# Issuing the last chunk's output projection and layer norm among the FFN matmuls of the chunk ahead of it

## The reference

```python
xn = _layernorm(x, axis=-1)
s = _L0_attn_ref(xn, L0_attn_w_qkv, L0_attn_w_out)      # global attention, 16 heads of 16
g = _silu(_L0_ffn_ref(xn, ...))                         # two local layers, below
x = x + s * g

def _layer(x, wqkv, qs, ksc, wo, lg, lb, w1, b1, w2, b2):   # applied DEPTH = 2 times
    h = shift_token(x)                       # the second half of the features comes from the token before
    q, k, v = split(h @ wqkv)                # 8 heads of 64
    q, k = rotary_xpos(l2norm(q) * qs, l2norm(k) * ksc)
    o = local_attention(q, k, v)             # windows of 128 tokens, each sees itself and the one before
    x = x + o @ wo                           # output projection
    h = shift_token(x)
    mu = h.mean(-1, keepdims=True)
    var = h.var(-1, keepdims=True)
    h = (h - mu) / jnp.sqrt(var + 1e-05) * lg + lb
    a, g = jnp.split(h @ w1 + b1, 2, axis=-1)
    x = x + (a * gelu(g)) @ w2 + b2          # hidden width 682: five tiles of 128 and a tail of 42
    return x
```

## Time and profile before

| what | us |
|---|---|
| median of 3 runs | 2339.86 (2337.14 to 2340.36) |
| the profiled execution's own time | 2328.96 |
| its span, first to last instruction | 2327.2 |
| mean granted TensorE clock | 0.971 of full speed |
| TensorE busy | 2195.7 (94%) |
| VectorE busy | 1621.7 (70%) |
| ScalarE busy | 1380.5 (59%) |

### The profile page before, as it was taken

One profiled execution on the slowest core, in us unless ns is written; L12 is line 12 of the kernel. 1 busy time (PEld: TensorE's weight loads), 2 busy tenths in 40 slices (PEclk: granted clock), 3 DMA queues, 4 the chain that ended last, 5 costly groups with the idle time before them and its releaser, 6 DMA issues. The chain is left out here.

```text
span 2327.2 us, 43427 instructions
## 1 busy us (share of the span) xinstructions
PE 2195.7 (94%) x14592; PEld 1288.5 (55%) x14592; DVE 1621.7 (70%) x3789; ACT 1380.5 (59%) x2551; POOL 610.5 (26%) x490
## 2 busy tenths in 40 slices
PE   7869999999999979899999999899999999999976
PEld 4533333333333336566666666666666676676644
DVE  5768999999999936655666666556666656666534
ACT  2215888888888845555655555555555565565533
POOL 3521200000000024333332333332432333333201
PEclk9977999999999989999999999999999999999988
DMA  4585122211112022200000000000100000000303
GB/s 135 183 252 159 52 64 65 65 56 60 57 53 63 29 80 103 88 10 1 1 0 0 0 0 0 27 1 10 36 1 1 1 0 0 0 0 0 108 1 109
DMA packets 76984, 108.96 MB, mean 47 GB/s; under 512 B 14204, under 2 KB 49360, under 8 KB 76752
## 3 DMA queue, kind: packets, MB, share of 16 engines
q1 hardware_dynamic: 76864, 107.30, 14.4%
HBM read 68.74 MB, written 43.95 MB: 48 GB/s over the span
## 5 line engine op out<-in xcount | busy, mean ns | idle before, releaser
L669 DVE TENSOR_REDUCE maxima<-ps_m 128x1 f32<-128x512 f32 x1024 | 629.1, 683 | 20.7 <-PE ps_m L549 16.6
L737 ACT ACTIVATE probs<-ps_st 128x1024 f32<-128x1024 f32 x512 | 521.1, 1025 | 161.7 <-PE ps_st L576 142.6
L549 PE MATMUL ps_m<-k_st,q_st 48*128 48x512 f32 x1024 | 392.4, 466 | 19.9 <-DMA k_st<-ks 15.6
L1355 ACT ACTIVATE l_probs<-l_probs,l_neg_max 128x256 f32<-128x256 f32 x512 | 254.0, 498 | 194.5 <-DVE l_neg_max L1514 194.5
L576 PE MATMUL ps_st<-q_st,k_st 50*128 50x512 f32 x1024 | 367.5, 444 | 2.0 <-DMA q_st<-max_rows 1.6
L592 PE MATMUL ps_o<-probs,v_st 128*32 128x256 f32 x4096 | 322.1, 392 | 0.1
L1514 DVE CUSTOM_DVE_ANT_1 l_probs<-ring,l_mask 128x256 f32<-128x256 f32 x384 | 140.0, 421 | 198.5 <-PE ring L1123 198.0
L576 PEld LDWEIGHTS ps_st<-q_st,k_st 50*128 50x128 f32 x1024 | 154.5, 186 | 194.0 <-issue 173.8
L1334 ACT COPY p_turned<-ring 128x512 f32<-128x512 f32 x256 | 140.4, 599 | 163.7 <-PE ring L1083 163.6
L1042 POOL TENSOR_SCALAR clipped<-sumsq 128x16 f32<-128x16 f32 x64 | 16.2, 253 | 766.9 <-DVE sumsq L1481 766.9
L549 PEld LDWEIGHTS ps_m<-k_st,q_st 48*128 48x128 f32 x1024 | 166.7, 190 | 53.3 <-DVE maxima L669 31.5
(11 more groups left out here) (156 smaller groups left out, 3864.7 us busy)
## 6 DMA issues: line engine op xcount, KB each, us to landing
qs<-split SPq DMA_DIRECT2D x16, 512.0 KB, 3.5
ks<-split SPq DMA_DIRECT2D x16, 512.0 KB, 5.1
q_st<-qs SPq DMA_DIRECT2D x64, 128.0 KB, 2.5
k_st<-ks SPq DMA_DIRECT2D x64, 128.0 KB, 3.1
o<-o_sb SPq DMA_DIRECT2D x32, 256.0 KB, 2.3
hidden<-o SPq DMA_DIRECT2D x17, 256.0 KB, 6.6
x_in<-in_L_attn_x_dram SPq DMA_DIRECT2D x8, 512.0 KB, 5.6
v<-v_sb SPq DMA_DIRECT2D x16, 256.0 KB, 4.7
```

Source lines behind the costliest of these rows:

```text
L549: nc.tensor.matmul(bank(base, use)[:, :], q_st[u][r, qt * P:(qt + 1) * P], k_st[u][r, h * CH:(h + 1) * CH], start=True, stop=True).then_in ...
L669: nc.vector.tensor_reduce(maxima[:, par, side(e), tile + e // 4, e % 2:e % 2 + 1], bank(base, k + e)[:, :], AX_X, ALU.max).then_inc(m_used, 1)
L737: nc.scalar.activation(probs[:, kt % 4, j, :], ps_st[j][:, :], ACT.Exp, scale=float(G_DIM) ** -0.5).then_inc(exp_done, 1)
L1355: nc.scalar.activation(probs[:, head, :], probs[:, head, :], ACT.Exp, bias=neg_max[:, head:head + 1], scale=-1.0, accum_out=total[:, head: ...
```

## The change

For body 17 (called late) the projection, the mean and the variance are issued in body 16, into `ps_q`, `ps_k`, `ps_v` and `l_ps_o`, which attention no longer uses there. Their other operands also get new places, all of them attention's: `mid` becomes a view of `l_probs`, `centred` becomes `qk_n`, the squares go to `k_ring`, and the features go to `h` instead of `f_high`/`f_low`. The counts of uses of the `ffn` banks are lowered by the two that fall away (`nth`). ScalarE's table preload goes in body 16 window 2 and in body 17. The arithmetic is the same.

```diff
+        late_banks = (ps_q, ps_k, ps_v, ps_o)
+        l_mid = probs.rearrange("p h n -> p (h n)")[:, 0:KD * (1 + CH)].rearrange("p (k n) -> p k n", k=KD)
+        l_centred, l_squares = qk_n[:, :, :], k_ring[:, 0:KD, :]
+        def late(g):
+            return isinstance(g, int) and g == LAST + 1
+        def nth(g, bank, use):
+            return (g - 2) * USES[bank] + use - (2 if late(g) else 0)
...
+                def late_fill(n, operands):
+                    for k, (a, b) in enumerate(operands):
+                        mm = nc.tensor.matmul(late_banks[n][:, :], a, b, start=(k == 0), stop=(k == len(operands) - 1))
+                    mm.then_inc(late_ready, 1)
+                def late_output():
+                    g = LAST + 1
+                    pe.wait_ge(o_out, WPC * (g - 1))
+                    pe.wait_ge(roped, WPC * LAST)
+                    for m in range(KD):
+                        late_fill(m, [(wt.wo[:, p, m * P:(m + 1) * P], o_ring[:, g % 2, p, :]) for p in range(HEADS // 2)])
+                def late_mean():
+                    pe.wait_ge(v_out, WPC * LAST)
+                    pe.wait_ge(late_mid, KD)
+                    late_fill(2, [(wt.mean_w[:, :], x) for x in shifted(l_mid)])
+                def late_variance():
+                    pe.wait_ge(sq_dev, LAST)
+                    late_fill(3, [(wt.mean_w[:, :], l_squares[:, k, :]) for k in range(KD)])
...
                         if forward and w == 2:
                             hidden_tile(g, lf, 3)
+                        if last_but_one and w == 2:
+                            late_output()
+                        if last_but_one and w == 3:
+                            late_mean()
                         if forward and w == 3:
                             down(g, lf, 0)
+                        if last_but_one and w == 3:
+                            late_variance()
...
-                        if w >= 2 and forward:
+                        if w >= 2 and forward and (mid_ or isinstance(g, int) and g == LAST and w == 3):
                             nc.scalar.preload_act_table_set(EXP_LN)
...
-                        if forward and w == 0:
+                        if forward and w == 0 and not late(g):
                             inverse_deviation(g)
+                        if isinstance(g, int) and g == LAST and w == 3:
+                            square_deviations(g + 1)
+                            inverse_deviation(g + 1)
...
+                        if last_but_one and w == 3:
+                            add_attention(g + 1, n + 1)
...
+                        if last_but_one and w == 3:
+                            centre(g + 1)
                         if forward and w == 3:
                             add_ffn(g, lf, n, 0)
+                        if last_but_one and w == 3:
+                            scale(g + 1, lf)
+                            shift(g + 1, lf)
+                        if forward and w == 3:
                             add_ffn(g, lf, n, 1)
                             carry(g, n)
```

More of the change, by code:

```diff
@@ L1186, in body @@
                 def body(g, la, lf, before_hidden=None):
+                    last_but_one = isinstance(g, int) and g == LAST
                     for w in range(WPC):
@@ L1541, in centre @@
-                def centre(g):
-                    dve.wait_ge(ffn_ready[0], (g - 2) * USES[0] + MEAN + 1)
-                    nc.vector.scalar_tensor_tensor(out=centred[:, 0, :], in0=ffn[0][:, :], scalar=-1.0, in1=mid[:, 0, 1:], op0=ALU.mult, op1=ALU.add)
-                    nc.vector.scalar_tensor_tensor(out=centred[:, 1, :], in0=ffn[0][:, :], scalar=-1.0, in1=mid[:, 1, 0:CH], op0=ALU.mult,
-                                                   op1=ALU.add).then_inc(ffn_taken[0], 1)
+                        if late(g):
+                            dve.wait_ge(late_ready, m + 1)
+                        else:
+                            dve.wait_ge(ffn_ready[m], (g - 2) * USES[m] + WO + 1)
@@ new lines, in add_attention @@
+                        ins = nc.vector.tensor_tensor(mid_of(g)[:, m, 1:], (late_banks if late(g) else ffn)[m][:, :], x_chunk(n, m, slice(1, 1 + CH)), ALU.add)
+                        ins.then_inc(late_mid if late(g) else ffn_taken[m], 1)
+                def centre(g):
+                    if late(g):
+                        dve.wait_ge(late_ready, 3)
+                    else:
+                        dve.wait_ge(ffn_ready[0], (g - 2) * USES[0] + MEAN + 1)
+                    bank = ps_v if late(g) else ffn[0]
+                    nc.vector.scalar_tensor_tensor(out=centred_of(g)[:, 0, :], in0=bank[:, :], scalar=-1.0, in1=mid_of(g)[:, 0, 1:], op0=ALU.mult, op1=ALU.add)
+                    nc.vector.scalar_tensor_tensor(out=centred_of(g)[:, 1, :], in0=bank[:, :], scalar=-1.0, in1=mid_of(g)[:, 1, 0:CH], op0=ALU.mult,
+                                                   op1=ALU.add).then_inc(late_centred if late(g) else ffn_taken[0], 1)
@@ L1598, in body @@
                             before_hidden()
-                        if forward and w == 1:
+                        if forward and w == 1 and not late(g):
                             scale(g, lf)
```

66 lines of the change are left out of this document (41 added, 25 removed).

## The result

The changed kernel took 2317.42 us (median of 7 runs, 2315.10 to 2323.94), and the kernel before 2338.93 (7 runs, 2328.62 to 2340.36). The ratio is 0.9933, with a 95% interval of 0.9915 to 0.9951: 15.7 us faster, between 11.5 and 19.9. (The two medians lie 21.5 us apart and the two means 17.1; what follows goes by the ratio, which has an interval.) The forecast was 2328.7 us in a range of 2324.5 to 2333.0, a gain of 11.2 us.

A forecast was written before the change was run, and what follows sets the result against it. It took latency of one chain at body 17's start (TensorE idle 9.88 us) as the bound, TensorE's pace elsewhere. First tile 9.7 us earlier plus 1.54 of clock gave 11.2: 2339.86 - 11.2 = 2328.7 us, range 2324.5 to 2333.

The forecast's parts named there:

- What bounds the kernel: At body 17's start one latency chain leaves TensorE idle 9.88 us; before and behind it TensorE's own pace binds.
- The slack of each late step: In body 16 each moved step comes in time: 3.5 us of slack for the mean, 2.5 for the variance.
- The last wait: Ahead of body 17's first tile TensorE waits 1.15 us for add_ffn 1, with bounds of 0.3 and 2.6.
- The clock: Body 17's tiles run at full speed from the start, 15.65 us instead of 17.19: 1.54 us more gain.
- the first rival: The stall ahead of body 17 costs the clock: gain 8.1 to 9.7 us, time 2330.2 to 2331.8; chance 0.12.
- The sum: Body 17's first tile 9.7 us earlier, plus 1.54 us of clock in its tiles: gain 11.2 us.
- The inserted matmuls: Projection, mean and variance placed in body 16 take 7.0, 1.8 and 1.9 us there, together 10.7 us.
- the table loads: Four removed ScalarE loads of 1.28 us in the two bodies, costed at nothing as lying under TensorE's tiles.
- carry the difference over as it is: Profiled execution is 10.90 us below the timed median; that difference is kept, so 2339.86 - 11.2 = 2328.7 us.
- The closing block: Its 28.80 us stay, give or take 1; a rival had transfers absorb the gain, time 2339.9, chance 0.04.
- the slower case: Clock falls before body 17's first tile and stays at 1.2 GHz through the body: 12 us slower, 2352; chance 0.02.
- rule on short idle spells: Short idle spells between matmul groups can make the clock swing; by it body 17's gain would be near 9.7 us.

The follow-up runs named there:

- e2_output_only: Changed kernel with only the output projection and add_attention kept in body 16, mean and all behind it back in body 17; ratio to before 0.9993.
- e3_add_first: Changed kernel with body 16's add_ffn 1 ahead of scale and shift on VectorE; ratio to before 0.9968.
- e4_swapped: Changed kernel with body 16's two down products and add_ffn in the other order, the variance issued inside the first product; ratio to before 0.9941.
- e5_ln5: Changed kernel with four idle Ln ahead of the late one; body 16's first tile to the last add_ffn took 67.30 us, against 63.45.
- e6_loads: Kernel before with only the table preloads removed, profiled only; body 16's first tile to the last add_ffn took 75.09 us, against 75.32.
- e12_loads5: Kernel before with only the table preloads removed, timed; ratio to before 1.0004, median 2336.21 us.
- e9_best: e4_swapped plus silu's table loaded behind body 17's last gate and no carry in body 17; ratio to before 0.9929, median 2320.91 us.
- e11_after: The changed kernel, unchanged, timed again against the kernel before; ratio 0.9932, median 2317.57 us.
- e10_wide: Changed kernel with 128x512 fp32 filler matmuls ahead of and among the score products at the start of global attention; profiled execution 2343.03 us.
- e8_warm: Changed kernel with 128x128 fp32 filler matmuls ahead of and among global attention's score products; ratio to before 1.0101, median 2356.68 us.

## Why the prediction was wrong

**What bounds the kernel, and the place of the gain: right.** The idle 9.88 us of the earlier trace rows are 1.16 after. e2_output_only shows that 8.1 of them (2.56 and 5.56) belong to the chain behind the projection, and only the other 1.8 to the projection.

**The slack of each late step: right.** Projection straight behind tile 3, no idle ahead of mean and variance, centre 0.20 after the start of the matmul behind the mean, the squares done at 2248.56 with the variance at 2251.04.

**The last wait: right.** 1.15 us forecast, 1.16 measured, released by `add_ffn` 1 as said. e3_add_first and e4_swapped, expected from the same working, came out within some 0.2 us (3.68 us against 3.7 for the wait; 1.22 against 1.0).

**The clock: right in kind.** It holds behind 1.16 us, so the first rival did not happen; behind 3.47 us (e5_ln5) and 4.83 us (e3_add_first) it did.

**The sum: 11.2 forecast, 11.87 measured.** Two terms were off. The inserted matmuls were put at 10.7 us; the starts give 3.43 for each half of the projection (2233.10 to 2236.53) and 1.72 each for mean and variance (2244.17 to 2245.89, 2251.04 to 2252.76), together 10.3. I had taken the tail off too little. And the table loads, put at nothing because they "lie under TensorE's tiles", are worth 0.2 us (e6_loads, e12_loads5). The two make up nearly all of the 0.67 us between forecast and trace.

**The step that failed** is the one that turned the gain into a time: "so I carry the difference over as it is: 2339.86 - 11.2". The 10.90 us between the profiled execution and the median of three were not an offset that belongs to profiling. They were two draws from one spread. In later runs the profiled execution lay anywhere among the timed ones: 1.8 us below the median for the changed kernel, 14.4 above it for e9_best, 4.6, 5.1 and 5.7 above it for e2, e3 and e4. The profiled execution of before had a short stretch at half speed (58.0 us), and the three timed ones lie between 2337.14 and 2340.36, where 76 executions have a median of 2333.0 and go down to 2324.2. The forecast took the upper edge of that spread as its base. By the same gain from 2333.0 it would have been 2321.8, and with the 11.87 of the trace 2321.1. So of the 11.3 us between forecast and measurement, 6.9 are the base, 0.7 the sum, and 3.7 are left: the draw of seven executions of the changed kernel, and what the profiles don't show of the gain. Even around 2321.8, the range as I had set it would have ended at 2317.6, just above the 2317.42 measured. The range (whose lower end is 2324.7 by its own terms, not 2324.5) allowed 3 us below and 1.2 us above for scatter, read off from three executions that happened to agree. Drawn from the 76, the medians of two sets of seven differ by 4 us (one standard deviation), and by more than 5.4 one time in five. The seven of before beside the result had a median of 2338.93, as high again; so high a median of seven comes from the 76 about one time in fifty, and whether that session had something of its own stays open. "The parts touched are short and run on one core's engines alone" was no argument either, since the spread goes with the mean clock, and in the profiles the clock differs 2000 us ahead of them.

**The ratio** of 0.9933 says 15.7 us where the trace says 11.87. Its interval holds the trace's number; the rest is taken up under e11_after and is settled only in part.

**The rivals.** The closing block gave nothing back (28.70 us against 28.77), and nothing of the slower case was seen. The Trainium skill's rule on short idle spells ("TensorE: Matmul & The Clock Gate", "A second HAM failure mode: psum-queue depth-cycling") is not borne out in body 17 for a spell of 1.16 us, behind which the granted clock stays at 1.00. At the start of e10_wide the clock did fall, 0.6 us behind a spell of 0.96 us, so the length of the spell does not settle it.

## What to carry to other kernels

Where a chain of short steps closes a kernel with nothing beside it, it can often be issued under the matmuls ahead of it, if buffers and banks of a finished stage are free; then look for the last wait, which can be for a bank given back late, as here, and not for the data. Put the gain together from one point in the program that both kernels reach by the same code, and keep it apart from the base. Before a time is forecast to 0.2%, ask what the same kernel's executions scatter by and where the profiled one lies among them: three that agree do not say.

## What the runs showed of the hardware that I had not expected

- The clock of TensorE fell while it was busy. In e8_warm no wait stood between the 128x128 fp32 fillers and the score products of 48 rows, and the products' distance went from 0.85 us (160.59 to 161.44) to 1.44 us (165.75 to 167.19); with fillers of 128x512 it stayed at full speed for the first 32 products, until 185.3, 0.6 us behind a wait of 0.96 us. So a fall needs no wait just ahead of it.
- The first matmuls behind a wait of 3.47 us ran at full speed, and the fall came 1 us later, in the middle of a tile (e5_ln5).
- With the same code ahead of it, body 16's first tile came between 2221 and 2233 us in eleven profiles and at 2245 in the twelfth, by how long the clock stayed low near the start.
